# A gated feed-forward block: the third cycle's gate as columns on 128x4 tiles, and the order of the work where two batches meet

## The reference, cut to what matters

```python
def ffn(x):                                  # x: layernorm of the residual stream
    gf = global_net(x.mean(axis=1))          # one number per batch
    out = x
    for _ in range(3):                       # three gating cycles
        h = gelu(out @ w1 + b1); h = gelu(h @ w2 + b2); h = gelu(h @ w3 + b3)
        tf = sigmoid(h @ w4 + b4)            # one number per row of x
        c = 0.1 + adaptive_range * (0.7 * gf + 0.3 * tf - 0.5) * 2.0
        o_r, o_i, p_r, p_i = split(out, 4)   # 128 features each
        out = out + c * concat(p_r, -p_i, -o_r, o_i)
    return out
y = x + tanh(g_ffn) * ffn(layernorm(x))
```

## Time and profile before

| | |
|---|---|
| device time, 3 runs | 1820.77 us median (1819.86 to 1821.71) |
| the profiled execution | 1819.01 us |
| its span, first to last instruction | 1817.2 us, mean granted TensorE clock 0.990 |
| start of batch 0's first transposes | 1304.24 us |
| end of VectorE's last operation | 1814.43 us |

### The profile page before, as it was taken

The page is one execution under the profiler, slowest core; times in us unless marked ns, Lnnn a source line. Parts: engine busy times, 40 slices in busy tenths (PEclk is TensorE's granted clock), DMA queues, the critical chain, the costliest instruction groups (busy, mean ns, idle before and its releaser), DMA issues. The chain is left out here.

```text
span 1817.2 us, 33693 instructions
## 1 busy us (share of the span) xinstructions
PE 1761.7 (97%) x12280; PEld 1274.7 (70%) x12280; DVE 1458.7 (80%) x2527; ACT 1220.3 (67%) x2121; POOL 653.2 (36%) x591
## 2 busy tenths in 40 slices
PE   7999999999999999999999999999999899899896
PEld 6888886777777777777777777777764664755752
DVE  5545555999999999999999999999658847847848
ACT  3222225999999999999999999999454344443542
POOL 3432423332387442586324864633242110110100
PEclk9999999999999999999999999999999999999998
DMA  8777666745478653667753777526315330330101
GB/s 263 264 252 281 249 231 171 169 144 129 130 186 180 135 138 94 181 172 134 164 120 100 206 164 151 116 73 174 104 47 174 107 93 1 107 93 0 61 1 46
DMA packets 152212, 254.60 MB, mean 140 GB/s; under 512 B 17024, under 2 KB 69504, under 8 KB 152064
## 3 DMA queue, kind: packets, MB, share of 16 engines
q1 hardware_dynamic: 101408, 157.73, 27.0%
q0 software_dynamic: 50080, 93.87, 23.4%
q10 hardware_dynamic: 576, 1.05, 0.2%
HBM read 168.44 MB, written 84.15 MB: 139 GB/s over the span
## 5 line engine op out<-in xcount | busy, mean ns | idle before, releaser
L967 DVE CUSTOM_DVE_ANT_0 a_neg<-a_sc_ps,am 128x1024 f32<-128x1024 f32 x512 | 621.1, 1213 | 1.3 <-PE a_sc_ps L820 1.3
L916 ACT ACTIVATE a_prob<-a_neg,a_row_min 128x1024 f32<-128x1024 f32 x512 | 586.6, 1146 | 7.7 <-DVE a_row_min L967 4.6
L832 PEld LDWEIGHTS a_tr_ps<-ident,a_prob 128*128 128x128 f32 x4096 | 460.4, 140 | 136.1 <-issue 100.3
L832 PE MATMUL a_tr_ps<-ident,a_prob 128*128 128x128 f32 x4096 | 545.8, 276 | 1.4 <-ACT a_probT L896 1.4
L942 DVE COPY a_probT<-a_tr_ps 128x512 f32<-128x512 f32 x512 | 353.8, 691 | 49.0 <-PE a_tr_ps L832 36.5
L896 ACT ACTIVATE a_probT<-a_tr_ps 128x512 f32<-128x512 f32 x512 | 305.6, 597 | 74.2 <-PE a_tr_ps L832 49.1
L1293 PE MATMUL f_acc<-f_u,f_w 128*128 128x512 f32 x384 | 173.5, 596 | 0.0
L716 POOL DMA_DIRECT2D a_q_st<-q_parts x144 | 79.4, 557 | 210.1 <-PE a_sc_ps L820 174.3
L853 PE MATMUL a_o_ps<-a_probT,v_first 128*32 128x256 f32 x2048 | 137.0, 385 | 0.0
L853 PE MATMUL a_o_ps<-a_probT,a_v 128*32 128x256 f32 x2048 | 136.4, 385 | 0.2 <-ACT a_probT L896 0.2
L1293 PEld LDWEIGHTS f_acc<-f_u,f_w 128*128 128x128 f32 x384 | 71.4, 190 | 90.7 <-issue 75.8
(11 more groups left out here) (202 smaller groups left out, 2964.0 us busy)
## 6 DMA issues: line engine op xcount, KB each, us to landing
a_q_st<-q_parts POOLq DMA_DIRECT2D x144, 128.0 KB, 2.9
k_first<-k_parts POOLq DMA_DIRECT2D x24, 512.0 KB, 7.8
a_k_st<-k_parts POOLq DMA_DIRECT2D x24, 512.0 KB, 7.5
a_m_raw<-mask SPq DMA_DIRECT2D x24, 512.0 KB, 5.2
a_adj_raw<-adj SPq DMA_DIRECT2D x24, 512.0 KB, 6.6
p_x_raw<-x POOLq DMA_DIRECT2D x8, 1024.0 KB, 7.4
k_parts<-p_out_hi SPq DMA_DIRECT2D x32, 256.0 KB, 3.2
k_parts<-p_out_lo SPq DMA_DIRECT2D x32, 256.0 KB, 5.6
```

The lines of the kernel that those rows point to most:

```text
L832: last = pe.transpose(tr_ps[:, half, j * P:(j + 1) * P], prob[:, r % NPROB, t * P:(t + 1) * P], ident[:])
L916: act.activation(prob[:, r % NPROB, :], neg[:, r % 2, :], ACT.Exp, scale=-1.0, bias=row_min[:, r % 2:r % 2 + 1], accum_out=row_sum[:, r // ...
L967: dve.tensor_tensor_reduce(out=neg[:, r % 2, :], in0=sc_ps[:, r % 2, :], in1=am[:, 2 * qb + qt, :], scale=-1.0, scalar=3.4e38, op0=ALU.add ...
```

## The change

In the third cycle `layer4` is replaced by `layer4_columns`: the activations h3 are the weights and `w4` the one moving column, four matmuls that give the logits as a 128x4 tile. `gate_columns` takes tanh of it, and `y_columns` computes c and the last step of (alpha, beta) on 128x4 tiles. What is turned by `columns` is now the pair (alpha, beta) of the second cycle, which ScalarE's `pack` copies into one tile at the end of turns 3 and 4; `columns(b, 0)` stands in turn 4 ahead of `layer3`, `columns(b, 1)` in turn 5 behind it.

All four `finish(b, 0, s)` stand in VectorE's turn 4. All eight projections of the next batch, its residuals and the four `finish(b, 1, s)` stand behind turn 5, in a new order; `residual(b, 1, 2)` is ahead of `split_x`. At the very end `finish_base` and `finish_add` share the last three output tiles with ScalarE's `twist` (twelve 128x128 copies scaled by a column).

```diff
@@ TensorE @@
+            def layer4_columns(b, j):
+                k = turn(b, CYCLES - 1, j)
+                pe.wait_ge(h3_ready, k + 1)
+                for s in range(TT):
+                    last = pe.matmul(tr[:, j, s:s + 1], h2[j][:, 0, s * P:(s + 1) * P], small.w4_col[:], start=True, stop=True)
+                last.then_inc(z4_ready, 1)
             def columns(b, j):
-                pe.wait_ge(coef_step, coef_steps(b, CYCLES - 1, j))
+                pe.wait_ge(packed, NJ * b + j + 1)
...
             def batch(b, first, more):
-                if first:
-                    project(b, 0, 0)
-                    project(b, 0, 1)
-                project(b, 0, 2)
-                project(b, 0, 3)
+                for s in range(TT):
+                    project(b, 0, s)
                 project(b, 1, 0)
-                if not first:
-                    columns(b - 1, 1)
                 project(b, 1, 1)
                 project(b, 1, 2)
-                if not first:
-                    pe.wait_ge(cols_ready, 2 * (NJ * (b - 1) + 1) + 2)
+                wait(pe, y_cols_step, 6 * NJ * b)
                 transpose_x(b, 0, 0)
...
-                    if k == NJ * CYCLES - 1 and more:
-                        project(b + 1, 0, 0)
-                        project(b + 1, 0, 1)
-                        columns(b, 0)
                     layer2(b, n, j, (1, 2, 3))
-                    if k == NJ * CYCLES - 1 and not more:
+                    if n == CYCLES - 1 and j == 0:
                         columns(b, 0)
                     layer3(b, n, j)
                     if k < NJ * CYCLES - 1:
                         layer2(b, (k + 1) // NJ, (k + 1) % NJ, (0,))
-                    layer4(b, n, j)
+                    else:
+                        columns(b, 1)
+                    if n < CYCLES - 1:
+                        layer4(b, n, j)
+                    else:
+                        layer4_columns(b, j)
@@ ScalarE @@
+            def gate_columns(b, j):
+                act.wait_ge(z4_ready, turn(b, CYCLES - 1, j) + 1)
+                act.activation(t_cols[:, j, :], tr[:, j, 0:TT], ACT.Tanh, scale=0.5, bias=small.half_b4[:]).then_inc(t_ready, 1)
+            def pack(b, j):
+                h = P // 2
+                act.wait_ge(coef_step, coef_steps(b, 1, j))
+                act.activation(coef[0:h, j, :], alpha[0:h, j, :], ACT.Copy)
+                act.activation(coef[h:P, j, :], beta[h:P, j, :], ACT.Copy).then_inc(packed, 1)
+            def twist(b, j, s):
+                act.wait_ge(y_cols_step, 6 * (NJ * b + j) + 6)
+                for t in range(ET):
+                    source, kind = ((2, 1), (3, 2), (0, 2), (1, 1))[t]
+                    last = act.activation(Bt[j][:, s, t * P:(t + 1) * P], xn[j][:, s, source * P:(source + 1) * P], ACT.Copy, scale=y_cols[:, j, kind, s:s + 1])
+                last.then_inc(twist_ready, 1)
@@ VectorE @@
+            def y_columns(b, j):
...
+                dve.wait_ge(t_ready, turn(b, CYCLES - 1, j) + 1)
+                dve.tensor_scalar(c, t_cols[:, j], small.range_3[:], base[:], ALU.mult, ALU.add).then_inc(y_cols_step, 1)
+                dve.wait_ge(cols_ready, k + 1)
+                dve.wait_ge(y_cols_step, done + 1)
+                dve.tensor_tensor(cross_be, c, be, ALU.mult).then_inc(y_cols_step, 1)
+                dve.tensor_tensor(cross_al, c, al, ALU.mult).then_inc(y_cols_step, 1)
+                dve.wait_ge(y_cols_step, done + 2)
+                dve.tensor_tensor(y_cols[:, j, 0], al, cross_be, ALU.subtract).then_inc(y_cols_step, 1)
+                dve.wait_ge(y_cols_step, done + 3)
+                dve.tensor_tensor(y_cols[:, j, 1], be, cross_al, ALU.add).then_inc(y_cols_step, 1)
+                dve.scalar_tensor_tensor(y_cols[:, j, 2], cross_al, -1.0, be, ALU.mult, ALU.subtract).then_inc(y_cols_step, 1)
+                dve.wait_ge(y_cols_step, done + 6)
...
             def batch(b, first, more):
-                if first:
-                    residual(b, 0, 0)
-                    residual(b, 0, 1)
+                finish_before(0)
+                residual(b, 0, 0)
+                finish_before(1)
+                residual(b, 0, 1)
                 residual(b, 0, 2)
                 residual(b, 0, 3)
                 mean_var(b, 0)
...
+                finish_before(2)
                 residual(b, 1, 0)
+                finish_before(3)
                 residual(b, 1, 1)
+                residual(b, 1, 2)
                 split_x(b, 0, 0)
                 split_x(b, 0, 1)
-                residual(b, 1, 2)
                 residual(b, 1, 3)
                 mean_var(b, 1)
...
-            for s in range(TT):
-                finish(B - 1, 1, s)
+            finish(B - 1, 1, 0)
+            finish_base(B - 1, 1, 1)
+            for s in range(2, TT):
+                finish_base(B - 1, 1, s)
+                finish_add(B - 1, 1, s - 1)
+            finish_add(B - 1, 1, TT - 1)
```

More of the change, by code:

```diff
@@ L1108, in ffn_phase @@
         cols_ready = sem("f_cols_ready")
+        packed = sem("f_packed")
+        y_cols_step = sem("f_y_cols_step")
+        twist_ready = sem("f_twist_ready")
         y_base = sem("f_y_base")
@@ L1363, in batch @@
                         layer2(b, (k + 1) // NJ, (k + 1) % NJ, (0,))
-                    layer4(b, n, j)
+                    else:
[4 more added lines that the diff above has]
+                        layer4_columns(b, j)
             batches(pe, batch)
-            columns(B - 1, 1)
         @block.scalar
@@ L1479, in batch @@
                         h1(*other, 1)
-                    gate(b, n, j)
+                    if n < CYCLES - 1:
+                        gate(b, n, j)
+                    else:
+                        gate_columns(b, j)
                     if between:
@@ L1483, in batch @@
                         h1(*other, 3)
+                        if other[1] == CYCLES - 1:
+                            pack(b, other[2])
             batches(act, batch)
+            for s in range(1, TT):
+                twist(B - 1, NJ - 1, s)
         @block.vector
@@ L1603, in finish, with finish_base @@
+            def finish_base(b, j, s):
+                dve.scalar_tensor_tensor(u[j][:, s, :], xn[j][:, s, :], y_cols[:, j, 0, s:s + 1], x1[j][:, s, :], ALU.mult, ALU.add).then_inc(y_base, 1)
             def finish(b, j, s):
                 k = TT * (NJ * b + j) + s
-                dve.scalar_tensor_tensor(u[j][:, s, :], xn[j][:, s, :], cols[:, j, 2 * s:2 * s + 1], x1[j][:, s, :], ALU.mult, ALU.add).then_inc(y_base, 1)
+                finish_base(b, j, s)
                 dve.wait_ge(y_base, k + 1)
@@ L1612, in finish, with finish_add, finish_before @@
                                                     u[j][:, s, t * P:(t + 1) * P], ALU.mult, ALU.add)
                 last.then_inc(y_ready, 1)
+            def finish_add(b, j, s):
+                dve.wait_ge(twist_ready, s)
+                dve.wait_ge(y_base, TT * (NJ * b + j) + s + 1)
+                dve.tensor_tensor(u[j][:, s, :], u[j][:, s, :], Bt[j][:, s, :], ALU.add).then_inc(y_ready, 1)
             def batch(b, first, more):
-                if first:
-                    residual(b, 0, 0)
-                    residual(b, 0, 1)
+                def finish_before(s):
+                    if not first:
+                        finish(b - 1, 1, s)
+                finish_before(0)
+                residual(b, 0, 0)
+                finish_before(1)
+                residual(b, 0, 1)
@@ L1623, in batch @@
                     prepare_weights()
-                else:
-                    gated_columns(b - 1, 1)
-                    finish(b - 1, 1, 0)
+                finish_before(2)
                 residual(b, 1, 0)
-                if not first:
-                    finish(b - 1, 1, 1)
+                finish_before(3)
                 residual(b, 1, 1)
-                if not first:
-                    finish(b - 1, 1, 2)
+                residual(b, 1, 2)
                 split_x(b, 0, 0)
                 split_x(b, 0, 1)
-                residual(b, 1, 2)
-                if not first:
-                    finish(b - 1, 1, 3)
                 residual(b, 1, 3)
@@ L1655, in batch @@
                     n, j = k // NJ, k % NJ
-                    coefficients(b, n, j)
                     if n < CYCLES - 1:
+                        coefficients(b, n, j)
                         mix(b, n + 1, j)
                     else:
+                        gated_columns(b, j)
+                        y_columns(b, j)
                         if j == 0:
-                            gated_columns(b, 0)
-                        finish(b, 0, 2 * j)
-                        finish(b, 0, 2 * j + 1)
-                        if j == 0 and more:
-                            residual(b + 1, 0, 0)
-                            residual(b + 1, 0, 1)
-            batches(dve, batch)
-            gated_columns(B - 1, 1)
-            for s in range(TT):
```

(6 more changed lines are left out.)

40 lines of the change are left out of this document (18 added, 22 removed).

## The result

The changed kernel takes 1787.32 us (median of four executions, 1783.96 to 1789.88), the kernel before 1821.24 beside it (four, 1819.86 to 1822.82). The ratio is 0.9817, with 95% between 0.9805 and 0.9830. The forecast was 1787.0. The profiled execution took 1788.19 us, its span 1786.3, mean granted TensorE clock 0.992.

The account below looks back on a forecast made before the run. TensorE was busy 97% of the span, so gains had to come from its waits, mostly paced by VectorE at boundaries. Boundaries and batch 0 (25.4 us) plus the end (8.4) took 33.8 from 1820.77: 1787.0, range 1784 to 1790, chance 0.68.

Parts of the forecast that it names:

- Turn 4 to turn 5: Batch boundary, layer 4 of turn 4 to that of turn 5: 9.6 us, 5.6 less, with `pack` hidden.
- The bound of 1.6 us for the two copies: `pack` on ScalarE: two copies take 1.6 us at most, hidden in 2.38 us of idle time.
- Turn 5 to the transposes: Layer 4 of turn 5 to the next batch's first transposes: seven projections, 20.2 us, no wait for `xn`.
- the 1.6 us of margin: Ahead of the first transposes: `xn` ready at 18.6 us behind layer 4 of turn 5, TensorE at 20.2.
- First to second transposes: Next batch's start: batch 0's 14.77 us less two waits, with 0.1 of VectorE lateness, 13.7 us.
- Rival (a): VectorE stays late at the boundaries, 1 to 4 us each: 1790 to 1799 us; chance 0.18, shared with a short clock fall.
- The end: Last turn: VectorE ends at 1805.7 instead of 1814.4; 8.4 us saved after queueing.
- the 0.3 given back to queueing: Kernel end: the last stores come 0.6 us apart, not 1.86, so 0.3 us of the saving is lost.
- (b): Only the end gains, the boundaries find another bound: 1812 us; chance 0.04, shared with anything up to 1817.
- (c): TensorE's clock falls behind turn 5's tiny products: 16 us slower than before, 1837; chance 0.02, shared with other losses.
- (d): Fewer clock falls than in the old kernel and more overlap at the end: 1782 us; chance 0.07 for under 1784.
- The signs: Trace checks: 43.5 us from layer 4 of turn 4 to second transposes, batch 0 13.6, the end 8.1, no `xn` wait.

Follow-up runs that it names:

- experiment 7: Changed kernel with four spare 64x512 copies on ScalarE ahead of each `pack`, into an idle tile: 1793.32 us, ratio 0.9846.
- Experiment 2: Changed kernel with the old 128x512 gate, keeping the new order at the boundaries; last batch ends as before the change: 1809.98 us, ratio 0.9952.
- experiment 1: Changed kernel keeping the 128x4 gate and new end, but with the old order where two batches meet: 1801.21 us, ratio 0.9905.
- experiment 4: Changed kernel with `residual(b, 1, 2)` put back behind `split_x(b, 0, 1)`: 1791.95 us, ratio 0.9848.
- experiment 3: Changed kernel with its last four finishes plain, without ScalarE's copies or the split into base and add: 1786.35 us, ratio 0.9816.

## Why the prediction was right

The time was 0.3 us beside the forecast, and each stage near its number:

| step of the prediction | forecast, us | measured, us |
|---|---|---|
| turn 4 to turn 5, its frame (8.89 + the 0.58 by which turn 4 came later) | 9.6 | 9.47 |
| layer 4 of turn 5 to first transposes | 20.2 | 20.09 |
| first to second transposes | 13.7 | 13.50 |
| the same in batch 0 | 13.6 | 13.44 |
| `layer4_columns`, its duration | 0.95 | 0.95 |
| the same against the old layer 4, start to start, turn 4 | +0.09 | -0.05 |
| `y_columns` | 0.9 | 0.94 |
| one of the twelve copies, start to start | 0.29 | 0.30 |
| layer 4 of turn 5 to VectorE's last operation | 8.1 | 8.05 |

**Turn 4 to turn 5.** Right: `pack` was hidden, and experiment 7 shows that the cover ends where the prediction drew it, at the wait of ScalarE for layer 2. The bound of 1.6 us for the two copies was 1.25 (0.62 + 0.63). `layer4_columns` lasted the row's 0.95, but the term made of it was mis-sized: the prediction set that duration beside the old layer 4's 0.86, which is read from start to start. From start to start `layer4_columns` takes 1644.16 - 1643.35 = 0.81 in turn 4, as `columns` did before (1794.88 - 1794.07), so the edit saved 0.05 us there and cost no 0.09. The sum hardly feels it. The estimate from the Trainium skill (TensorE: Matmul & The Clock Gate, "LDWEIGHTS (loading the stationary operand)") was 0.85, between the two readings, 0.81 from start to start and 0.95 as a duration.

**Turn 5 to the transposes.** Right: seven projections in a row, no wait for `xn`. The last statistics of the first half end 1665.84 - 1652.24 = 13.6 us behind layer 4 (13.5 forecast). Experiment 2 shows that the 1.6 us of margin came from the short gate: with the old one the wait is 3.17.

**First to second transposes.** Right, and experiments 1 and 4 part its reasons: the old order costs 17.85 - 13.50 = 4.35 us here, and residual (1, 2) behind `split_x` is 1.3 of that. Rival (a), VectorE late by 1 to 4 us, did not come: `split_x` starts as early as it can. By taking batch 0's piece, which had no fall of the clock, the prediction also counted the 0.8 us of the clock at two boundaries without naming it.

**The end.** Right at the operations; 8.64 us of the span (8.4 forecast). Of the 0.3 given back to queueing 0.1 was taken: the span ends 2.89 us behind VectorE's last operation, where before it was 2.8. How much of it is the gate and how much the two moved finishes was counted in one and is not parted by a run (experiment 3).

**The rivals.** (b) falls with the boundary table. (c), the clock behind turn 5, did not come: no stretch from turn 5 to the second transposes is under full clock. But the argument against it was wrong as a rule. "1.84 us of one-column products stand amid first-layer matmuls that keep their pace" was true of the execution of before (and of experiment 1); the same products were followed by a fall in two of the four batches in three profiled executions of after and in experiment 3, and in one batch in experiments 2, 4 and 7. A fall cost 1.6 us and not the 17 of the worst case. Of (d) a part came: the three falls at the boundaries went, and two others came.

**The signs.** The prediction named 43.5 us from layer 4 of turn 4 to the second transposes; the trace has 42.5, since 0.6 us of `columns(b, 0)` had moved out of that frame into turn 3 to turn 4. With it, it is 43.1.

**The sum.** The stages gave 35.7 us (boundaries 25.6, batch 0 1.3, the end 8.7 with the 0.1 of its last turns), 1.9 more than the 33.8 forecast; the clock in batches 2 and 3 took back 3.2, and batch 0 started 1.6 later. So in the profiled spans it was 30.9 and the hit of the median to 0.3 us is partly luck: the profiled execution of before lay 2.2 us under its median, that of after 0.9 over. Why the first transposes of batch 0 start anywhere from 1303.0 to 1307.0 us in kernels whose code up to there is alike stays open; no run was made on it. Open too is what decides in which batches the context products bring the clock down.

## What to carry to other kernels

When an engine's order is rebuilt, look for a stage of the same kernel that already runs without the obstacle (here batch 0): its piece was the right forecast to 0.2 us. A quantity that is alike on all partitions or needed once per row belongs in a 128x4 tile as soon as nothing full-sized needs it: 0.16 us an operation instead of 0.7. And judge a change of 1 or 2 us by its stage, landmark to landmark; the boundary of after repeated to 0.05 us (52.79 to 52.84 in three profiled executions), while whole executions of it differed by up to 6.6 us within one run.

## What the runs showed of the hardware

- One-column fp32 products can lower TensorE's clock although TensorE shows no gap: eight of them in a row (16 matmul records, 1.84 us) were followed by a fall in 11 of 36 batches (0.70 and 0.75 granted in the stretches behind), sixteen in a row in all four batches, and two groups of four in none of eight. A fall behind eight products cost 1.6 us. What decides between one batch and the next is not shown.
- The same fall costs nothing where a wait follows it: at the boundary of batches 2 and 3 of before it shortened a wait from 2.06 to 0.61 us, at the other two it stood behind the last wait and cost 0.8 us.
- Four 128x128 operations of VectorE in a row cost 1.14 us alone and 4.08 beside GpSimd's reads of SBUF, each ending about 0.14 us behind the end of a GpSimd instruction. One GpSimd `tensor_scalar` of 128x512, begun beside a two-input operation of VectorE on 128x512, took 1.24 us, the next 0.73. Work handed to GpSimd at the end (4.5 us of it) made the end 1.8 us longer.
- A chain of six VectorE operations on 128x4 tiles with a semaphore wait between most of them takes 0.94 us from its first start to the start of what needs it.
- ScalarE's 128x128 copies with a column as scale last 0.39 us each and follow each other every 0.30 us. The page ScalarE: Activation LUTs of the Trainium skill ("Rules for kernel authors") would give an estimated 0.41 for one, near the duration; back to back they overlap.
